# Last angles in halves, turned rows and input projection by pairs of batches, one table set for sine and SiLU, ahead of the state-space loop

## The chip, the core and the metric

The kernel runs on one core of one Trainium2 chip. The metric is the time of one execution on the device in microseconds (us), taken as the median of several runs. A core has five engines with an instruction stream each: TensorE (PE, matrix multiply; weight loads are listed apart as PEld), VectorE (DVE), ScalarE (ACT), GpSimd (POOL) and SyncE (SP, which issues the transfers here). Each runs its stream strictly in program order; they wait for each other on semaphores. Matmul results land in eight banks of PSUM, 512 float32 columns each, numbered 0 to 7.

## The reference, cut to what matters

Two decoder layers on `x` (8 batches of 128 tokens, 128 wide), each with three residual blocks followed by a layer norm. Layer 0: a gated delta-rule attention, a cross-attention on a context, and a feed-forward with a sine. Layer 1: a state-space block, a cross-attention with folded projections, and a gated feed-forward. The change lies between the sine feed-forward and the state-space block:

```python
# layer 0, feed-forward: 512 hidden features
hidden = x @ W1 + b1
imag = w_imag * sin(theta + hidden * 0.1)
phase = cos(theta) * w_real + sin(theta) * w_imag
x = layernorm(x + relu(hidden + phase * imag * 0.1) @ W2 + b2)
# layer 1, state-space block: 256 inner features, 16 states
xp, z = split(x @ W_in + b_in)
u = silu(xp)
Bm, Cm = split(u @ W_x + b_x)
dt = softplus(u @ W_dt + b_dt)
# scan over the 128 tokens: h = h * exp(dt * A) + dt * u * B ; y = h . C + D * u
y = y * silu(z)
x = layernorm(x + y @ W_out + b_out)
```

## The kernel before

Every engine's stream is written out by hand, with waits on named semaphores (`wait_ge`), so the order in the source is the order on the engine. The 8 batches are worked in two halves of four, g = 0 and g = 1; a half has 4 x 128 = 512 columns, one bank.

**The sine feed-forward.** The hidden features are made in four blocks k = 0 to 3, each of two parts m = 0, 1 of 512 columns: blocks 0 and 1 are the features of half 0, blocks 2 and 3 those of half 1. PE writes block k to two banks (`s3_banks` = 0, 4, 6, 2 is the first of each). ACT's `angle(k)` turns them into turns (angle by 2 pi) in `s3_ang[:, k]`. The sine wants its argument within one turn, so DVE's `fraction(k)` takes the fractional part in two operations over 1024 columns: an add of the constant ROUND, and a subtraction of the whole part. ACT's `sine(k)` takes the sine in place, and DVE's `gate3(k)` combines it with the hidden features. `rectified` applies the relu, PE's `project3(g, bank)` multiplies by W2 and adds the residual in a bank.

**The norm between.** For a half, DVE's `landed(3, g, bank)` waits for the projection and takes mean and variance (`bn_stats`, `bn_aggr`, then `veps`), POOL's `power(3, g)` raises variance plus epsilon to the power -0.5 (one small instruction on 128x4, tile `rstd`), and DVE's `normal(3, g, bank)` writes the four normalized batches to `xrow`, one instruction each.

**Into the state-space block.** PE's `turn_half(3, 0)` transposes the four batches as each is normalized, all to one bank. ACT's `columns_out(3, 0)` copies that bank to `xcol` in one instruction. PE's `project4` multiplies by W_in, once for each of the two halves of the inner features (n = 0, 1), to banks 4 and 5. ACT's `inner(n, ...)` applies SiLU to `u4`. PE's `steps(0, bank, n)` makes the step sizes and `narrow` the rows B and C. Then come the pieces of softplus on ACT (abs, exp, relu, ln) and DVE, and the loop over 64 steps q: DVE's `drive_of` (L681) and `scan_of` (L688), ACT's `fading`, POOL's `read_out` (L1052), PE's `widen_b` (L1751) and `accumulate` (L1767). A normalized half 1 follows inside the loop.

**Tables.** ACT's functions come in table sets, and an `ACT_TABLE_LOAD` changes the set. `table_of(f)` issues a tiny activation of function f, so that the load for it stands where that call stands. Where a function that isn't in the current set comes without such a call, the compiler puts the load ahead of it.

The line numbers of the profile are those of the kernel before; the changed kernel's are 10 to 23 higher. This is what DVE does before:

```python
            fraction(2)
            landed(3, 0, 0)
            fraction(3)
            normal(3, 0, 0)
            gate3(2)
            gate3(3)
```

## Time and profile before

| | |
|---|---|
| median of 3 runs | 390.78 us (390.59 to 390.94) |
| the profiled execution | 391.07 us, of which 388.8 us are the span from the first to the last instruction |
| busy in the span | PE 318.3 us (82%), DVE 310.2 (80%), ACT 213.7 (55%), POOL 217.0 (56%) |
| mean granted TensorE clock | 0.943 of full speed |

The profiled execution is one run; its time is 0.29 us above the median, and 2.27 us of it lie outside the span. Busy shares are means over very different stages: until some 119 us the first attention and the cross-attention, until 157 us the sine feed-forward and the beginning of the state-space block, until about 272 us the loop, and then the last cross-attention and feed-forward. In a timeline row, merged instructions stand as one with their count (for PE two records make one float32 matmul of the forms here, save the 128-column transposes, which have one), and the bracket says how long the engine was idle just before and what released it. Neighbouring instructions of an engine overlap by some hundredths of a us.

### The profile page before, as it was taken

What the parts mean: (1) busy time and instruction counts of PE and PEld (TensorE: products, weight loads), DVE (VectorE), ACT (ScalarE), POOL (GpSimd) and SP (SyncE); (2) the same over time, 40 slices, a digit from 0 to 9 for tenths busy, and PEclk for the clock granted to TensorE, in tenths of its full rate; (3) what the DMA queues carried; (4) which work ended last, traced back from release to release, by engine and by line L of the source; (5) the groups of instructions that cost most, each with busy time, mean ns of one, the idle gap of its engine ahead of it and who ended that gap; (6) DMA issues with size and microseconds to landing.
All of it is one profiled execution on the core that took longest, in us unless ns stands there. A gap on an engine that the chain in (4) does not pass through costs nothing. (4 is left out here: it accounts for less than half of the span.)

```text
span 388.8 us, 5449 instructions
## 1 busy us (share of the span) xinstructions
PE 318.3 (82%) x1750; PEld 234.4 (60%) x1750; DVE 310.2 (80%) x630; ACT 213.7 (55%) x468; POOL 217.0 (56%) x223
## 2 busy tenths in 40 slices
PE   5636929779768889867976997978899989999992
PEld 2432419778546465634434985555698857989872
DVE  0799999998676977989999999999958724763934
ACT  2726131222135859857759636787465657675741
POOL 3399999997133050478999999888602610100111
PEclk9956968999999999979998799999999999999998
DMA  8900000000000001334534443543200000000010
GB/s 238 418 35 1 0 3 0 2 1 2 0 0 2 1 0 36 124 112 132 158 121 156 141 142 118 155 136 135 81 3 0 0 2 0 3 1 2 0 29 27
DMA packets 11522, 24.43 MB, mean 63 GB/s; under 512 B 1231, under 2 KB 2255, under 8 KB 11239
## 3 DMA queue, kind: packets, MB, share of 16 engines
q1 hardware_dynamic: 11495, 24.09, 18.9%
q8 instruction: 14, 0.23, 0.2%
q14 instruction: 13, 0.11, 0.1%
HBM read 23.50 MB, written 0.59 MB: 62 GB/s over the span
## 5 line engine op out<-in xcount | busy, mean ns | idle before, releaser
L1052 POOL TENSOR_TENSOR arena<-arena 128x512 f32<-128x512 f32 x63 | 80.1, 1281 | 27.8 <-DVE arena L688 25.8
L688 DVE TENSOR_TENSOR_SCAN arena<-arena,ps 128x512 f32<-128x512 f32 x64 | 77.3, 1209 | 0.1
L1311 ACT ACTIVATE arena<-arena,neg_a 128x508 f32<-128x508 f32 x64 | 43.2, 712 | 9.2 <-DVE arena L688 7.1
L681 DVE TENSOR_TENSOR ps<-arena,ps 128x512 f32<-128x512 f32 x64 | 43.2, 676 | 1.2 <-PE ps L1751 1.1
L1767 PE MATMUL ps<-first_in,arena 128*128 128x128 f32 x256 | 41.4, 286 | 3.2 <-POOL arena L1052 3.1
L1093 POOL TENSOR_TENSOR rstd<-veps,mhalf 128x4 f32<-128x4 f32 (+2 forms) x6 | 4.8, 810 | 68.8 <-DVE veps L803 35.8
L1585 PE MATMUL ps<-arena,first_in 128*128 128x128 f32 (+1 forms) x256 | 31.9, 287 | 12.7 <-POOL arena L926 12.7
L715 DVE TENSOR_REDUCE arena<-ps 128x2 f32<-128x496 f32 x32 | 21.4, 668 | 25.1 <-PE ps L1813 25.0
L1767 PEld LDWEIGHTS ps<-first_in,arena 128*128 128x128 f32 x256 | 33.0, 147 | 13.7 <-POOL arena L1052 6.5
L1585 PEld LDWEIGHTS ps<-arena,first_in 128*128 128x128 f32 x256 | 30.8, 201 | 14.0 <-issue 8.1
L1751 PE MATMUL ps<-arena,pick_wide 96*128 96x512 bf16 x64 | 25.5, 404 | 16.7 <-DVE arena L688 16.2
L1361 ACT ACTIVATE first_in<-ps 128x256 f32<-128x256 f32 x32 | 12.4, 387 | 33.2 <-PE ps L1839 33.1
L1347 ACT ACTIVATE arena<-ps,arena 128x248 f32<-128x248 f32 x64 | 29.4, 472 | 0.9 <-DVE arena L715 0.8
L1751 PEld LDWEIGHTS ps<-arena,pick_wide 96*128 96x128 bf16 x64 | 6.4, 100 | 35.4 <-DVE arena L688 32.6
L1813 PE MATMUL ps<-kvT,arena 128*128 128x248 f32 x96 | 24.2, 375 | 0.0
L939 POOL TENSOR_TENSOR rstd<-veps,mhalf 128x4 f32<-128x4 f32 x8 | 8.6, 1074 | 24.4 <-DVE veps L701 16.3
L1188 ACT ACTIVATE arena<-arena 128x64 f32<-128x64 f32 x15 | 6.2, 413 | 28.5 <-DVE arena L539 28.5
L926 POOL TENSOR_TENSOR arena<-arena 128x512 f32<-128x512 f32 x16 | 20.6, 1289 | 0.3
L1850 PEld LDWEIGHTS ps<-fold_vo,first_in 128*128 128x128 f32 x128 | 18.4, 191 | 3.8 <-ACT first_in L1361 2.1
L1850 PE MATMUL ps<-fold_vo,first_in 128*128 128x128 f32 x128 | 19.6, 279 | 1.2 <-ACT first_in L1361 0.5
L724 DVE TENSOR_TENSOR arena<-arena 128x496 f32<-128x496 f32 x28 | 19.6, 700 | 1.0
L1355 ACT ACTIVATE arena<-ps 128x512 f32<-128x512 f32 x32 | 19.2, 600 | 1.2 <-PE ps L1827 0.2
(290 smaller groups left out, 809.8 us busy)
## 6 DMA issues: line engine op xcount, KB each, us to landing
arena<-c_rows_dram SPq DMA_DIRECT2D x64, 256.0 KB, 3.2
fold_in<-in_fold_dram SPq DMA_DIRECT2D x1, 2056.0 KB, 11.9
late_in<-in_late_dram SPq DMA_DIRECT2D x1, 1423.5 KB, 17.2
early_in<-in_early_dram SPq DMA_DIRECT2D x1, 921.5 KB, 13.7
xres<-in_x_dram SPq DMA_DIRECT2D x1, 512.0 KB, 14.2
kv_ctx<-in_context_dram SPq DMA_DIRECT2D x1, 480.0 KB, 7.8
first_in<-in_first_dram SPq DMA_DIRECT2D x1, 465.0 KB, 3.9
rows_in<-in_rows_dram SPq DMA_DIRECT2D x1, 384.0 KB, 14.7
```

The costliest lines, as they stand in the source:

```text
L681: tt(chain(q), dtu[:, n, cols(g)], chain(q), ALU.mult).then_inc(S("drive"), 1)
L688: nc.vector.tensor_tensor_scan(hist[:, q % NBUF], fade[:, q % NFADE], chain(q), 0.0, ALU.mult, ALU.add).then_inc(S("scan"), 1)
L715: nc.vector.tensor_reduce(s5_max[:, u % 2], sim, AX.X, ALU.max, negate=True).then_inc(S("sim_max"), 1)
L926: tt(prod_s[:, :, c % NR].rearrange("p j t i -> p t i j"), Qg[:, c].unsqueeze(2).to_broadcast([P, C, DH, DH]), state[:, c].unsqueeze(1).to ...
L1052: tt(seen[:, q % NBUF], hist[:, q % NBUF], c_wide[:, q % NBUF], ALU.mult).then_inc(S("read_out"), 1)
L1311: act(fade[:, q % NFADE].rearrange("p (b t) -> p b t", t=T)[:, :, 1:], dt[:, n, cols(g)].rearrange("p (b t) -> p b t", t=T)[:, :, 1:], ACT ...
L1347: act(s5_p[:, u % 2, h], sim_bank(u)[:, h * 256:h * 256 + KV], ACT.Exp, bias=s5_max[:, u % 2, h:h + 1], accum_out=s5_den[:, u % 2, h:h + 1 ...
L1585: ins = mm(bank(6 + c // NR)[:, at:at + n_c * C * DH], ident, pr[:, j, c % NR:c % NR + n_c].rearrange("p c t i -> p (c t i)"), start=(n == ...
L1751: mm(chain(q), pick[:, s], bc_parts[0:96, cols(g)], start=True, stop=True).then_inc(S("b_mm"), 1)
L1767: ins = mm(y_bank(p // NS)[:, b * T:(b + 1) * T], seen[:, p % NBUF, b * T:(b + 1) * T], ident, is_transpose=True, start=False, stop=last a ...
L1813: ins = mm(sim_bank(u)[:, i * 256:i * 256 + KV], s5_q[b // HB][h + i][:, b % HB * T:(b % HB + 1) * T], kvT[:, b], start=True, stop=True)
L1850: ins = mm(out5_bank(b), s5_z[:, u % 4, i * T:(i + 1) * T], fold_vo[:, h + i], start=(h + i == 0), stop=(h + i == XH - 1))
```

## The change

Five edits. DVE: the last block of angles is made fractional by its two halves of columns, one half ahead of `landed(3, 0, 0)`, one in the old place. ACT: a `table_of(Silu)` stands ahead of the first sine, and the one after the last sine is gone; the last sine is taken in two halves. PE and ACT: the four transposes of half 0 go by pairs to banks 4 and 1, and each pair is copied to `xcol` by itself. PE: W_in is applied to one pair after the other, 256 columns at a time. PE, ACT and DVE: the first step sizes go to bank 0 in place of bank 3, so that their matmuls wait for the gates up to the sixth only, while `narrow` behind them waits for all eight; the filler matmuls `stay_awake` behind them write bank 3 in place of bank 0.

```diff
--- before.py
+++ after.py
@@ -633,13 +633,23 @@
                     ts(s3_act[1][:, f], s3_ang[:, k, m * 512:(m + 1) * 512], W("b1")[:, f:f + 1], 0.0,
                        ALU.add, ALU.max).then_inc(S("act3_second"), 1)
 
+            def last_fraction(m):
+
+                ve.wait_ge(S("angle"), 7 + m)
+                ve.wait_ge(S("fraction"), 2 + m)
+                at = slice(m * 512, (m + 1) * 512)
+                whole, turns = s3_t[:, 1, at], s3_ang[:, 3, at]
+                then(ts(whole, turns, ROUND, None, ALU.add))
+                stt(turns, whole, ROUND, turns, ALU.subtract, ALU.subtract).then_inc(S("fraction"), 1)
+
             fraction(0)
             fraction(1)
             gate3(0)
             gate3(1)
             fraction(2)
+            last_fraction(0)
             landed(3, 0, 0)
-            fraction(3)
+            last_fraction(1)
             normal(3, 0, 0)
             gate3(2)
             gate3(3)
@@ -667,7 +677,7 @@
             b_low(0)
             ve.wait_ge(S("dt_lost"), 1)
             ve.wait_ge(S("dt_relu"), 1)
-            then(tt(dt[:, 0, h0], bank(3), dtu[:, 0, h0], ALU.subtract))
+            then(tt(dt[:, 0, h0], bank(0), dtu[:, 0, h0], ALU.subtract))
             ve.wait_ge(S("dt_log"), 1)
             tt(dt[:, 0, h0], bank(5), dt[:, 0, h0], ALU.add).then_inc(S("dt"), 1)
             ve.wait_ge(S("dt"), 1)
@@ -1227,6 +1237,7 @@
             act(na, na, ACT.Copy, scale=-1.0).then_inc(S("neg_a"), 1)
             mixed0(0)
             ac.wait_ge(S("theta"), 1)
+            table_of(ACT.Silu)
             act(s3_sin, s3_th, ACT.Sin).then_inc(S("theta_sin"), 1)
             turned0(1)
             mixed0(1)
@@ -1263,9 +1274,14 @@
             rectified(1)
             angle(3)
             sine(2)
-            sine(3)
-            columns_out(3, 0)
-            table_of(ACT.Silu)
+            for m in range(2):
+                ac.wait_ge(S("fraction"), 4 + m)
+                ins = act(s3_ang[:, 3, m * 512:(m + 1) * 512], s3_ang[:, 3, m * 512:(m + 1) * 512], ACT.Sin, scale=-2 * PI_F)
+            ins.then_inc(S("sine"), 1)
+            for m in range(2):
+                ac.wait_ge(S("turned"), 2 * B + 2 * (m + 1))
+                act(xcol[:, 2 * m:2 * m + 2], bank(4 - 3 * m)[:, 0:2 * T].rearrange("p (b t) -> p b t", b=2),
+                    ACT.Copy).then_inc(S("xcol"), 1)
 
             def inner(n, g, k):
 
@@ -1315,10 +1331,10 @@
             for n in range(NH):
                 inner(n, 0, 4 + n)
             table_of(ACT.Exp)
-            step_abs(0, 3, bank(4))
+            step_abs(0, 0, bank(4))
             step_exp(0, bank(4))
             rows_b(0, 2)
-            step_relu(0, 3, bank(3))
+            step_relu(0, 0, bank(0))
             table_of(ACT.Ln)
             ac.wait_ge(S("dt_lost"), 1)
             step_log(0, bank(5), bank(4))
@@ -1715,10 +1731,16 @@
                 mm(bank(k), W("w_in")[:, n * P:(n + 1) * P], xcol[:, g * HB:(g + 1) * HB],
                    start=True, stop=True).then_inc(S(sem), 1)
 
-            turn_half(3, 0)
-            pe.wait_ge(S("xcol"), 5)
-            for n in range(NH):
-                project4(n, 0, 4 + n, "u_mm")
+            for b in range(HB):
+                pe.wait_ge(S("normed"), normed(3, b + 1))
+                turn(bank(4 - b // 2 * 3)[:, b % 2 * T:(b % 2 + 1) * T], xrow[:, 1, b], ident).then_inc(S("turned"), 1)
+            for m in range(2):
+                pe.wait_ge(S("xcol"), 5 + m)
+                for n in range(NH):
+                    ins = mm(bank(4 + n)[:, 2 * m * T:2 * (m + 1) * T], W("w_in")[:, n * P:(n + 1) * P], xcol[:, 2 * m:2 * m + 2],
+                             start=True, stop=True)
+                    if m:
+                        ins.then_inc(S("u_mm"), 1)
             wx = W("w_x").rearrange("p (n s) -> p n s", n=NH)
             wdt = W("w_dt").rearrange("p (n d) -> p n d", n=NH)
 
@@ -1728,11 +1750,12 @@
             def steps(m, k, n):
                 return mm(bank(k), wdt[:, n, m % 2 * P:(m % 2 + 1) * P], u4[:, n, cols(m // 2)], start=(n == 0), stop=(n == NH - 1))
 
-            pe.wait_ge(S("gated"), 2 * NF)
+            pe.wait_ge(S("gated"), 6)
             for n in range(NH):
                 pe.wait_ge(S("u_in"), n + 1)
-                ins = steps(0, 3, n)
+                ins = steps(0, 0, n)
             ins.then_inc(S("dt_mm"), 1)
+            pe.wait_ge(S("gated"), 2 * NF)
             for n in range(NH):
                 ins = narrow(0, 2, n)
             ins.then_inc(S("xdbl_mm"), 1)
@@ -1884,7 +1907,7 @@
             for n in range(NH):
                 ins = steps(1, 6, n)
             ins.then_inc(S("dt_mm"), 1)
-            stay_awake(4, 0)
+            stay_awake(4, 3)
             pe.wait_ge(S("diag_d"), NH)
             for q in range(NQ):
                 if q + 2 < NQ:
@@ -1901,7 +1924,7 @@
                     pe.wait_ge(S("dt_relu"), 2)
                     turn_half(3, 1)
                 if q == 6:
-                    pe.wait_ge(S("xcol"), 6)
+                    pe.wait_ge(S("xcol"), 7)
                     pe.wait_ge(S("fold_vo"), 2)
                 if q in (6, 7):
                     project4(q - 6, 1, q - 2, "u_mm")
```

On DVE, between the fractions of block 2 and the gates of blocks 2 and 3. Before:

```order
L620 TENSOR_SCALAR arena<-arena 128x1024
L621 SCALAR_TENSOR_TENSOR arena<-arena 128x1024
L416 BN_STATS stats<-ps 128x6 x4
L419 BN_AGGR mv<-stats 128x2 x4
L396 TENSOR_SCALAR veps<-mv 128x4
L620 TENSOR_SCALAR arena<-arena 128x1024
L621 SCALAR_TENSOR_TENSOR arena<-arena 128x1024
L425 TENSOR_SCALAR xrow<-ps,mv,rstd 128x128 x4
L628 SCALAR_TENSOR_TENSOR arena<-arena,s_cf,ps 128x512 x4
```

And now (L642 and L643 are the two operations of `last_fraction`):

```order
L620 TENSOR_SCALAR arena<-arena 128x1024
L621 SCALAR_TENSOR_TENSOR arena<-arena 128x1024
L642 TENSOR_SCALAR arena<-arena 128x512
L643 SCALAR_TENSOR_TENSOR arena<-arena 128x512
L416 BN_STATS stats<-ps 128x6 x4
L419 BN_AGGR mv<-stats 128x2 x4
L396 TENSOR_SCALAR veps<-mv 128x4
L642 TENSOR_SCALAR arena<-arena 128x512
L643 SCALAR_TENSOR_TENSOR arena<-arena 128x512
L425 TENSOR_SCALAR xrow<-ps,mv,rstd 128x128 x4
L628 SCALAR_TENSOR_TENSOR arena<-arena,s_cf,ps 128x512 x4
```

The last 1024-column pair (L620, L621) has become two 512-column pairs, one of them ahead of the statistics (L416).

On ACT, from the last angles (L1240) to the first piece of softplus (L1287). Before:

```order
L1240 ACTIVATE arena<-ps,s_bias 128x512 x2
L1252 ACTIVATE arena<-arena 128x1024 x2
L1111 ACTIVATE xcol<-ps 128x512
L1105 ACT_TABLE_LOAD
L1105 ACTIVATE table<-first_in 128x1
L1273 ACTIVATE arena<-ps,late_in 128x512 x2
L1105 ACT_TABLE_LOAD
L1105 ACTIVATE table<-first_in 128x1
L1287 ACTIVATE ps<-ps,late_in 128x512
```

And now, from the last angles (L1251) on:

```order
L1251 ACTIVATE arena<-ps,s_bias 128x512 x2
L1263 ACTIVATE arena<-arena 128x1024
L1279 ACTIVATE arena<-arena 128x512 x2
L1283 ACTIVATE xcol<-ps 128x256 x2
L1289 ACTIVATE arena<-ps,late_in 128x512 x2
L1115 ACT_TABLE_LOAD
L1115 ACTIVATE table<-first_in 128x1
L1303 ACTIVATE ps<-ps,late_in 128x512
```

The load and the one-column activation between the copy to `xcol` and the two SiLU (L1273 before, L1289 now) are gone; the sine (L1252) of block 3 has become two of 512 columns (L1279), and the copy (L1111) two of 256 (L1283). The load ahead of the first sine is now followed by one such one-column activation.

On PE, from the transposes to `steps` (L1729 before, L1751 now) and `narrow` (L1726, L1748), with the semaphores that they wait for. Before:

```order
L1541 MATMUL ps<-first_in,xrow 128x128 [waits normed] x4
L1715 MATMUL ps<-xcol,late_in 128x512 [waits xcol]
L1715 MATMUL ps<-xcol,late_in 128x512
L1729 MATMUL ps<-arena,late_in 128x512 [waits u_in,gated]
L1729 MATMUL ps<-arena,late_in 128x512 [waits u_in]
L1726 MATMUL ps<-arena,late_in 32x512 x2
L1604 MATMUL ps<-xres,first_in 128x512 [waits residual]
```

And now:

```order
L1736 MATMUL ps<-first_in,xrow 128x128 [waits normed] x4
L1740 MATMUL ps<-xcol,late_in 128x256 [waits xcol]
L1740 MATMUL ps<-xcol,late_in 128x256
L1740 MATMUL ps<-xcol,late_in 128x256 [waits xcol]
L1740 MATMUL ps<-xcol,late_in 128x256
L1751 MATMUL ps<-arena,late_in 128x512 [waits u_in,gated]
L1751 MATMUL ps<-arena,late_in 128x512 [waits u_in]
L1748 MATMUL ps<-arena,late_in 32x512 [waits gated]
L1748 MATMUL ps<-arena,late_in 32x512
```

Two projections of 512 columns (L1715) have become four of 256 (L1740), the third with a wait of its own, all four behind the fourth transpose; the first `narrow` has a wait.

## Rows read from the trace of the kernel before

**Rows 1.** Page, the 40 slices: granted TensorE clock in tenths of full speed, 9.72 us each

```profile
...
PEclk9956968999999999979998799999999999999998
```

**Rows 2.** Windows: us, then busy us (xinstructions) of five engines, granted clock, DMA share, GB/s

```profile
...
139.20:147.00 7.80, 6.60 (x24) 3.84 (x23) 7.63 (x21) 3.84 (x6) 5.38 (x6) 1.00 0.00 0
170.00:172.00 2.00, 1.19 (x7) 0.70 (x5) 2.00 (x3) 0.82 (x2) 2.00 (x3) 0.51 0.07 24
195.00:271.70 76.70, 64.78 (x370) 45.53 (x369) 76.12 (x101) 52.51 (x98) 70.16 (x63) 0.96 0.43 138
271.70:388.80 117.10, 105.60 (x627) 87.93 (x625) 71.22 (x183) 67.78 (x205) 21.85 (x27) 0.98 0.04 12
```

**Rows 3.** Page, costliest groups: total busy, mean ns of one | idle before, releaser

```profile
...
L688 DVE TENSOR_TENSOR_SCAN arena<-arena,ps 128x512 f32<-128x512 f32 x64 | 77.3, 1209 | 0.1
...
L1361 ACT ACTIVATE first_in<-ps 128x256 f32<-128x256 f32 x32 | 12.4, 387 | 33.2 <-PE ps L1839 33.1
```

**Rows 4.** Timeline: start us, us, engine line op xcount [idle before <-releaser]

```profile
...
136.32 1.25 ACT L1240 ACTIVATE arena<-ps,s_bias 128x512 f32<-128x512 f32 x2
...
138.91 3.62 PE L1535 MATMUL ps<-first_in 128*128 128x256 f32 x16
139.12 0.89 DVE L416 BATCH_NORM_STATS2 stats<-ps 128x6 f32<-128x128 f32 x4 [2.32 <-PE ps L1698]
...
140.54 0.69 DVE L620 TENSOR_SCALAR arena<-arena 128x1024 f32<-128x1024 f32 x1
140.71 1.40 POOL L939 TENSOR_TENSOR rstd<-veps,mhalf 128x4 f32<-128x4 f32 x1 [0.28 <-DVE veps L396]
141.26 1.23 DVE L621 SCALAR_TENSOR_TENSOR arena<-arena 128x1024 f32<-128x1024 f32 x1
...
142.41 1.36 DVE L425 TENSOR_SCALAR xrow<-ps,mv,rstd 128x128 f32<-128x128 f32 x4
142.52 1.06 ACT L1252 ACTIVATE arena<-arena 128x1024 f32<-128x1024 f32 x1 [4.02 <-DVE arena L621]
...
142.87 1.28 PE L1541 MATMUL ps<-first_in,xrow 128*128 128x128 f32 x4 [0.33 <-DVE xrow L425]
...
143.80 2.72 DVE L628 SCALAR_TENSOR_TENSOR arena<-arena,s_cf,ps 128x512 f32<-128x512 f32 x4
...
144.19 0.60 ACT L1111 ACTIVATE xcol<-ps 128x512 f32<-128x512 f32 x1 [0.61 <-PE ps L1541]
144.80 1.28 ACT L1105 ACT_TABLE_LOAD   x1
...
144.84 1.98 PE L1715 MATMUL ps<-xcol,late_in 128*128 128x512 f32 x4 [0.69 <-ACT xcol L1111]
...
146.21 1.34 ACT L1273 ACTIVATE arena<-ps,late_in 128x512 f32<-128x512 f32 x2
146.56 1.68 DVE L633 TENSOR_SCALAR arena<-arena,late_in 128x512 f32<-128x512 f32 x4
...
147.02 1.95 PE L1729 MATMUL ps<-arena,late_in 128*128 128x512 f32 x4 [0.20 <-ACT arena L1273]
...
149.01 0.66 ACT L1287 ACTIVATE ps<-ps,late_in 128x512 f32<-128x512 f32 x1
```

**Rows 5.** Instructions by tile, rstd: ns min/median/max

```profile
...
L939 POOL TENSOR_TENSOR rstd<-veps,mhalf x8: 1018/1029/1397, 103.3 to 297.1; 128x4 f32<-128x4 f32 x8
```

**Rows 6.** Timeline, around 92 us, the end of the first attention stage

```profile
...
92.01 1.05 DVE L327 TENSOR_TENSOR arena<-arena 128x512 f32<-128x512 f32 x1
92.06 0.97 POOL L957 TENSOR_SCALAR s_th<-late_in 128x4 f32<-128x4 f32 x1
```

**Rows 7.** Timeline, around 119 us, the load ahead of the first sine

```profile
...
118.92 1.28 ACT L1230 ACT_TABLE_LOAD   x1
...
120.58 0.60 ACT L1211 ACTIVATE arena<-ps 112x512 f32<-112x512 f32 x1 [0.17 <-PE ps L1649]
```

**Rows 8.** Timeline, DVE in the state-space loop

```profile
...
177.38 0.69 DVE L681 TENSOR_TENSOR ps<-arena,ps 128x512 f32<-128x512 f32 x1 [0.82 <-PE ps L1751]
```

## Prediction

> **What bounds the kernel now.** I read the windows first, then who waits in the stretch that the change touches. In the loop the bound is DVE: from 195 to 271.7 us it is busy for 76.12 of 76.70 us [rows 2], and its 64 scans waited 0.1 us in all [rows 3]. Behind the loop it is PE, busy for 105.60 of 117.10 us [rows 2]. Neither is touched, and both start from what came before, so any time won or lost ahead of the loop should arrive at the end unchanged. Ahead of it, from 139.2 to 147.0 us, DVE is busy for 7.63 of 7.80 us [rows 2], but only its first half stands in the way of others: the gates behind the normal are not waited for at once. PE's 6.60 us [rows 2] hold 3.62 us of filler matmuls at 138.91 [rows 4]. What sets the end here is a chain that goes from engine to engine. In the timeline [rows 4] it runs: statistics at 139.12 (DVE sat idle for 2.32 us before them), then the power on POOL at 140.71 beside DVE's last fractions (L620, L621); the normal at 142.41 (L425); transposes from 142.87; one copy to `xcol` at 144.19; W_in from 144.84; SiLU at 146.21; step sizes (L1729) at 147.02; the absolute value (L1287) at 149.01. From there on the order on every engine is as before.
>
> I call the start of the normal N. Before, N = 142.41 and the absolute value starts at N + 6.60. The change can win in both parts.
>
> **Part one: N, by the angles in halves.** The 1024-column pair at 140.54 and 141.26 ends at 142.49 and is what the normal waits for: it starts at 142.41, neighbours on an engine overlapping by 0.08 [rows 4]. A half costs 0.42 for the first operation (1.68 us for four scalar operations of 512 columns, L633) and 0.68 for the second (2.72 for four of L628, which read one operand from PSUM; the 1.23 us of L621 halved with the same fixed part gives the same within 0.02) [rows 4]. The early half goes into the idle 2.32 us: its angle, the first of the two of L1240, is there at about 137.0, so it ends at about 138.2, 0.9 us before the statistics. It costs nothing; without that cover it would cost 1.1. The late half runs from 140.54 to about 141.68. DVE could thus start the normal at 141.60.
>
> Now POOL is late. Its power ran from 140.71 to 142.11 [rows 4]; it took 1.40 us where the median of eight is 1.03 [rows 5]. The excess, 0.37, fits a wait behind L620, which ended at 141.23: the power would have asked for its operands some 0.15 us after its start. That such waits exist is seen in [rows 6], where a POOL operation on 128x4 stood for 0.97 us and ended with the DVE operation beside it. With the half operation ending at 140.96 the wait shrinks to 0.1 and the power ends at 140.71 + 1.13 = 141.84; with nothing in its way it ends at 141.74, with the old 1.40 at 142.11. Adding 0.03 for the signal, N = 141.87, bounds 141.77 and 142.14. Part one wins **0.54 us** (0.27 to 0.64).
>
> The Trainium skill (SBUF — State Buffer, Two separate sides) says that VectorE and GpSimd share a pair of ports by an exclusive lock, held for a whole instruction, taken by a VectorE operation in a two-port mode or by one with two SBUF inputs. The 1.40 and the 0.97 agree with that. It speaks against this change in one way: L621 and L643 have two SBUF inputs, and if L643 gets the ports first, the power waits for its end; the first rival below prices this.
>
> **Part two: from N to the absolute value.** The four normals end 0.34 us apart (1.36 for four). Before, the transposes start at N + 0.46 and take 0.32 each, the last ends at N + 1.74, the copy runs from N + 1.78 to N + 2.38, and W_in starts at N + 2.43 [rows 4]. By pairs: the second transpose ends at about N + 1.10, the copy of 256 columns costs 0.39 [rows 3], so the first pair is in `xcol` at N + 1.53. All four transposes stand ahead of W_in on PE, the last ending at N + 1.74, but starting at N + 1.42, so W_in starts at N + 1.58 to 1.74. I take 1.58, since pipelined neighbours overlap. The second copy starts at N + 1.78 and ends at N + 2.17, ahead of the third projection. ACT is free for them: the late half of the sine costs less than the whole 1.06 [rows 4] and starts at 141.7, so it is done by about 142.4, and the first copy is due at 143.0.
>
> W_in itself costs the same columns. Two projections of 512 took 1.98 us (L1715) [rows 4], four passes of 0.43 and 0.26 until the result is there. The filler of 256 columns took 3.62 for 16 passes (L1535), 0.21 each with the same 0.26. So eight passes take 1.94; the first SiLU's operand is complete after six, at N + 1.58 + 1.52 = N + 3.10, the second's at N + 3.52. ACT starts SiLU at about N + 3.15, where it started at N + 3.80 before. Here the table counts: before, the load (1.28 us from 144.80) and the tiny activation behind it (0.13, until 146.21) ended later than the first projection, ready at 144.84 + 0.86 + 0.26 = 145.96. Alone, the removed load would win those 0.25 for the first SiLU, and almost nothing for the second (its operand was ready at 146.82, and it started at about 146.88). With the pairs, both move.
>
> From the first SiLU on, the distances hold: its 0.67, then the step sizes 0.14 later, 1.95 us for them, and on ACT 2.80 us from the start of the first SiLU to the absolute value (146.21 to 149.01, with two SiLU of together 1.34 and the table of Exp between) [rows 4]. ACT and PE reach this point together, at N + 5.95, where it was N + 6.60. The step sizes now wait for the gates up to the sixth (about N + 2.8), and `narrow` for all eight (N + 4.11; the four gates take 2.72 from N + 1.39), both ahead of need. Had bank 3 and the wait for eight stayed, the gates would still end at N + 4.11, at most 0.15 after the first SiLU at N + 3.82: that edit alone is worth 0.15 at most. Part two wins **0.65 us** (0.49 with W_in at N + 1.74).
>
> The Trainium skill (ScalarE: Activation LUTs, What ACT_TABLE_LOAD costs) gives 1.28 us for a load, as here, plus 1.38 for a drain. No drain of that size shows here: SiLU followed the load's end by 0.13 [rows 4]. By the page's 2.66 us ACT would be freed for longer, but the sum would stay, since PE's projection is what is waited for then.
>
> **What is added.** The load ahead of the first sine now has the tiny activation behind it, 0.13. ACT had 0.17 idle before its next copy (L1211) [rows 7], so ACT loses nothing. POOL's coefficients from that sine, and behind them on its stream the power of the block before, can be up to 0.13 later, and the second norm with it, unless PE covers it. I take **-0.05** (0 to -0.13). Bank 0 in place of 3, and the filler in the other bank, cost nothing, since reads and writes keep their sizes and order.
>
> **The sum.** 0.54 + 0.65 - 0.05 = 1.14 us. The profiled execution's 391.07 (388.8 in the span, 2.27 around it) would become 389.93; it stood 0.29 over the median, so for the median of 390.78 I say **389.65 us**. The likeliest case's own range is 389.4 to 390.0 (0.27 + 0.49 - 0.13 = 0.63 takes all bounds at once and belongs to the second rival).
>
> **The rivals.**
> - *The power falls behind L643.* If POOL asks after 140.96, the second operation has the operands' way, until 141.68; what the power had left at 141.23 before (until 142.11, 0.88) then ends at 142.56. N = 142.59, 0.18 later than before. 0.65 - 0.18 - 0.05 = 0.42 won: 390.35. For it: the margin, 0.25 us after POOL's start, is small. Against it: in the same place before, the power got through between L620 and L621. Chance 0.13.
> - *Both parts win at their lower ends*, the power staying at 1.40 us and W_in behind the last transpose: 0.63 to 0.76 won, 390.05 to 390.15. For it: nothing shows that the 1.40 came from L620. Chance 0.12.
> - *TensorE's clock falls elsewhere.* From about 170 us the granted clock was 0.51 [rows 2], 1.2 GHz in place of 2.4, for nearly one slice [rows 1], after a stretch in which PE had waited much; DVE waited for PE 0.82 us at 177.38 [rows 8]. If this interval shrinks as the stages shift, 0.8 us or a little more is won on top: about 388.8. Chance 0.06.
> - *It is slower.* The one mechanism that could do it is that same low clock in the chain before the loop, between 143 and 149 us: eight passes of 0.21 and four of 0.43 on the chain would double, +3.4 us, and 392 to 393 would result. It decides from about 2 us, half of the interval. Against it: the clock was 1.00 from 139.2 to 147.0 [rows 2], and PE waits less there after the change. Chance 0.05.
> - That the table's load isn't saved is excluded: the compiled order shows one load fewer and none between sine and SiLU.
>
> **How the numbers follow.** The forecast has 0.64. A measurement of this kernel tells about 0.2% (0.78 us) from no change. Faster by more than that: nearly all of the forecast, the clock's case and a little of the second rival, 0.71. Within: the first rival and most of the second, 0.23. Slower: 0.06. The range 389.1 to 390.4 holds forecast and both rivals, and leaves out the two of the clock.
>
> **What would show it.** The early fractions stand in the gap at about 137.1 to 138.2, and the statistics still start at 139.1. The power takes 1.0 to 1.15 us, and the normal starts at 141.9. The copies start 0.64 apart, W_in at N + 1.6, SiLU at N + 3.15, the absolute value at N + 5.95, that is at 147.8. The first scan, and then every later stage, is earlier by the same 1.1 us. It is wrong if the power is longer than 1.3 us, if the chain behind 149 us gives time back, or if the low clock moves.

## Result, and the profile after

The changed kernel takes **388.47 us** (median of 6 runs, 387.89 to 389.17), the kernel before 390.73 us in the same comparison (6 runs): a ratio of 0.9945, 95% interval 0.993 to 0.996, that is 1.6 to 2.7 us less. The forecast was 389.65 with a range of 389.1 to 390.4: the direction was right, the gain (2.26 us in place of 1.13) twice as large, and the time lies below the range. The profiled execution took 388.73 us, with a span of 386.5 in place of 388.8.

The chain ahead of the loop, from the timeline of the changed kernel (columns as in [rows 4], which hold the same places of before):

```profile
...
137.01 0.43 DVE L642 TENSOR_SCALAR arena<-arena 128x512 f32<-128x512 f32 x1 [0.22 <-ACT arena L1251]
...
137.47 0.69 DVE L643 SCALAR_TENSOR_TENSOR arena<-arena 128x512 f32<-128x512 f32 x1
...
139.10 0.89 DVE L416 BATCH_NORM_STATS2 stats<-ps 128x6 f32<-128x128 f32 x4 [0.94 <-PE ps L1714]
...
140.53 0.43 DVE L642 TENSOR_SCALAR arena<-arena 128x512 f32<-128x512 f32 x1
140.69 1.14 POOL L949 TENSOR_TENSOR rstd<-veps,mhalf 128x4 f32<-128x4 f32 x1 [0.28 <-DVE veps L396]
140.99 0.69 DVE L643 SCALAR_TENSOR_TENSOR arena<-arena 128x512 f32<-128x512 f32 x1
...
141.87 1.36 DVE L425 TENSOR_SCALAR xrow<-ps,mv,rstd 128x128 f32<-128x128 f32 x4 [0.18 <-POOL rstd L949]
...
142.36 1.26 PE L1736 MATMUL ps<-first_in,xrow 128*128 128x128 f32 x4
...
143.01 0.38 ACT L1283 ACTIVATE xcol<-ps 128x256 f32<-128x256 f32 x1 [0.67 <-PE ps L1736]
...
143.45 1.99 PE L1740 MATMUL ps<-xcol,late_in 128*128 128x256 f32 x8
143.65 0.38 ACT L1283 ACTIVATE xcol<-ps 128x256 f32<-128x256 f32 x1 [0.25 <-PE ps L1736]
145.05 1.27 ACT L1289 ACTIVATE arena<-ps,late_in 128x512 f32<-128x512 f32 x2 [1.01 <-PE ps L1740]
...
145.88 1.95 PE L1751 MATMUL ps<-arena,late_in 128*128 128x512 f32 x4 [0.44 <-ACT arena L1289]
...
147.88 0.66 ACT L1303 ACTIVATE ps<-ps,late_in 128x512 f32<-128x512 f32 x1
```

N, the start of the normal, is 141.87 where it was 142.41; the power took 1.14 us in place of 1.40. The first half of the fractions stands in the old gap, and the statistics start where they did, with 0.94 us idle ahead of them in place of 2.32. From N: W_in 1.58 later (2.43 before), SiLU 3.18 (3.80), the absolute value 6.01 (6.60).

The remaining gain of these two profiles lies in the loop. Below are the starts of a few of its scans in the two profiles, q counted from 0 (merged from the timelines; the third column is the difference):

```
 q    before   after    gain
 0    157.46   156.32   1.14
 8    175.35   174.18   1.17
 9    177.99   175.89   2.10
10    179.70   177.60   2.10
14    186.53   184.60   1.93
35    225.14   223.20   1.94
36    227.93   225.64   2.29
62    278.24   275.95   2.29
```

At the first scan the gain is the forecast's 1.14. It jumps by 0.93 at q = 9, falls by 0.17 up to q = 14, jumps by 0.35 at q = 36, and holds in between and from there to the end. The page of the changed kernel shows the granted clock (40 slices of 9.66 us; compare [rows 1]):

```profile
...
PEclk9955968999999999988997999999999999999997
```

and the windows show it finer (columns as in [rows 2]):

```profile
...
170.00:174.00 4.00, 4.00 (x13) 2.39 (x14) 3.76 (x5) 2.98 (x4) 4.00 (x5) 0.58 0.45 125
174.00:178.00 4.00, 3.30 (x17) 1.64 (x16) 4.00 (x6) 3.95 (x5) 4.00 (x4) 1.00 0.37 102
178.00:182.00 4.00, 2.49 (x14) 1.76 (x12) 4.00 (x5) 2.81 (x6) 3.87 (x4) 0.77 0.63 196
182.00:186.00 4.00, 4.00 (x16) 1.86 (x15) 3.94 (x6) 2.79 (x6) 4.00 (x4) 0.80 0.38 105
```

Before, TensorE ran at half clock (1.2 GHz) from about 170 to 177 us, and DVE waited for it, 0.82 us at 177.38 alone [rows 8]. In this execution of the changed kernel the low clock lasted from about 170 to 173.4 and came again from 180.2 to 183.7. Of the waits for TensorE in front of the drive one of 0.24 us is left. The jump at q = 36 comes long after another stretch of 6.8 us at half clock, which both have: it ended at about 217.9 before and at 214.4 now. Before, DVE waited 0.38 us for TensorE at 226.7, now it doesn't; what ties this wait to a low clock is not shown.

### The profile page after: what moved, and what is told of

The parts are those of the page before. It is cut to its first block and busy times, and to the rows that moved or that the text cites. A ratio compares the mean times of both kernels' runs of the same rounds, so it can differ in the third digit from the quotient of the medians.

```text
span 386.5 us, 5462 instructions
## 1 busy us (share of the span) xinstructions
PE 318.1 (82%) x1754; PEld 235.0 (61%) x1754; DVE 310.5 (80%) x632; ACT 212.7 (55%) x469; POOL 216.7 (56%) x223
```

## Experiments

For the runs below, the span of each profile is cut at the start of the statistics (L416), at scan 0, at scan 36 and at scan 62. Behind scan 0 all kernels have one order, save the fillers of the awake ones. Indented lines are further executions of the kernel above them. The profiles come from several chips.

```
                    statistics  to      to      to      to
                    start       scan 0  q = 36  q = 62  the end  span
kernel before       139.12      18.34   70.47   50.31   110.56   388.8
  before_again      137.76      19.61   69.36   50.31   110.56   387.6
  before_look1      139.18      18.35   68.89   50.31   110.57   387.3
  before_look2      139.09      18.34   70.55   50.30   110.52   388.8
awake_before        138.22      19.60   69.35   50.30   110.53   388.0
before_filled       139.52      18.34   68.92   50.31   110.51   387.6
  filled_look1      138.32      18.34   69.94   50.29   110.51   387.4
  filled_look2      139.69      18.34   68.94   50.30   110.53   387.8
table_only          138.26      18.15   70.46   50.31   110.52   387.7
halves_only         139.19      17.81   69.03   50.30   110.47   386.8
all_but_halves      139.26      17.75   69.06   50.30   110.53   386.9
changed kernel      139.10      17.22   69.32   50.31   110.55   386.5
  after_again       138.38      17.21   68.88   50.30   110.53   385.3
  after_look1       139.44      17.21   69.28   50.31   110.56   386.8
  after_look2       138.43      17.21   69.01   50.31   110.54   385.5
awake_after         138.08      17.22   68.92   50.89   110.49   385.6
  awake_filled      138.18      17.21   68.93   50.31   110.47   385.1
after_old_table     139.24      17.60   69.16   50.31   110.49   386.8
after_bank3         137.78      17.40   70.44   50.31   110.47   386.4
after_delayed       139.21      18.45   70.40   50.30   110.54   388.9
```

**Both parts by themselves.** `halves_only` is the kernel before with the fractions and the last sine in halves; `all_but_halves` is the changed kernel without them, its reverse. On the kernel before:

```diff
             fraction(2)
+            last_fraction(0)
             landed(3, 0, 0)
-            fraction(3)
+            last_fraction(1)
...
-            sine(3)
+            for m in range(2):
+                ac.wait_ge(S("fraction"), 4 + m)
...
```

> The kernel before with the last fractions and the last sine in halves, nothing else. Chain: the normal at 141.87 in place of 142.41, the power 1.14 in place of 1.40 us, every distance behind it as before, the first scan at 156.9 (0.54 earlier). Theory: the time is 0.54 us lower, plus or minus what the low clock stretches in the loop do, about 390.2, within 389.2 to 390.6. Rival (parts need each other, ScalarE is what is waited for): first scan earlier by less than 0.2.

> The changed kernel with the last fractions and the last sine whole again: pairs, one table set and bank 0 stay. The normal at 142.4 as before, SiLU 3.2 us behind it in place of 3.8, the absolute value 6.0 in place of 6.6, the first scan 0.6 earlier, at 156.85. Theory: 0.6 us lower, plus or minus the low clock stretches, about 390.1 (389.0 to 390.5). Rival (the halves free ScalarE, and without them the late sine, until 143.6, holds up the first copy, due at 143.5): 0.5 or less.

Measured: 389.63 us (12 runs; ratio 0.9967, 0.995 to 0.9984) and 389.34 us (0.997, 0.9955 to 0.9984). On the way to scan 0 the first wins 0.53 us (17.81 against 18.34), the second 0.59 (17.75); together 1.12, which is what the whole change wins there. `halves_only`, timeline:

```profile
...
140.61 0.43 DVE L642 TENSOR_SCALAR arena<-arena 128x512 f32<-128x512 f32 x1
140.78 1.14 POOL L949 TENSOR_TENSOR rstd<-veps,mhalf 128x4 f32<-128x4 f32 x1 [0.27 <-DVE veps L396]
...
141.95 1.36 DVE L425 TENSOR_SCALAR xrow<-ps,mv,rstd 128x128 f32<-128x128 f32 x4 [0.18 <-POOL rstd L949]
...
145.75 1.34 ACT L1286 ACTIVATE arena<-ps,late_in 128x512 f32<-128x512 f32 x2
...
148.56 0.66 ACT L1300 ACTIVATE ps<-ps,late_in 128x512 f32<-128x512 f32 x1
```

The power is short again, 1.14 us, beside the half operation, and 1.40 in `all_but_halves` beside the whole one. So the parts add up, and neither needs the other. The medians are 1.1 and 1.4 us under that of the kernel before (390.72), each twice its share of the chain. The intervals just leave out the shares of the chain alone, so each half seems to bring some of the part beyond it.

**The pieces of part two.** `table_only` moves the SiLU table ahead of the first sine and nothing else; `after_old_table` is the changed kernel with the tables as before; `after_bank3` is the changed kernel with the step sizes in bank 3 and their wait for all eight gates. The first diff is `table_only` on the kernel before (`after_old_table` is its reverse on the changed kernel), the second `after_bank3` on the changed kernel, its fillers back in bank 0 too:

```diff
+            table_of(ACT.Silu)
             act(s3_sin, s3_th, ACT.Sin).then_inc(S("theta_sin"), 1)
...
             columns_out(3, 0)
-            table_of(ACT.Silu)
```

```diff
-            pe.wait_ge(S("gated"), 6)
+            pe.wait_ge(S("gated"), 2 * NF)
...
-                ins = steps(0, 0, n)
+                ins = steps(0, 3, n)
```

> The kernel before with the one table set alone: SiLU no longer waits for its load. The first SiLU at N + 3.6 in place of 3.80 (W_in's first result), the second at N + 4.45 as before, the absolute value at N + 6.5 to 6.6 where the clock is full. Theory: 0 to 0.1 us on the chain, and the low stretch near 144 us may still come: within 0.3 of the kernel before. Rival (the table is the larger part of the gain): the absolute value at N + 6.2 or earlier.

> The changed kernel with the old tables: a load ahead of the first sine and one behind the last copy, ahead of SiLU. The second copy ends at N + 2.16, the load and its activation take 1.41, SiLU at N + 3.58 in place of 3.18, the absolute value at N + 6.4 in place of 6.01. Theory: 0.4 us slower than the changed kernel, about 388.9, first scan at 17.62 us behind the statistics in place of 17.22. Rival (the load costs a drain of over 1 us beside it): the absolute value at N + 7 or later.

> The changed kernel with the first step sizes in bank 3 again, so that they wait for all eight gates. The last gate ends at 145.99 and the first SiLU at 145.72 in the changed kernel; the step sizes start at 146.1 in place of 145.88, the absolute value at 148.05 to 148.1, 0.2 later. Theory: 0.1 to 0.25 us slower than the changed kernel on the chain, the first scan at 156.5. Rival (nothing waits there): the first scan at 156.32.

Measured: 390.28 us (ratio 0.9977, 0.9955 to 0.9998), 389.27 (0.9944, 0.9916 to 0.9972) and 389.03 (0.9955, 0.9935 to 0.9974). On the way to scan 0 the table alone wins 0.19, where 0 to 0.1 had been expected; taking it out of the changed kernel costs 0.39, and taking bank 0 and the early wait out costs 0.19. In `table_only` the absolute value comes at N + 6.56, only 0.04 earlier, as expected. But the chain doesn't run through it: the step sizes start at N + 4.42 in place of 4.61, `narrow` behind them is earlier by the same 0.19, and a later activation of ACT (L1282, the rows B) waits for `narrow`:

```profile
...
149.80 0.68 ACT L1282 ACTIVATE arena<-ps,late_in 32x512 f32<-32x512 f32 x1 [0.43 <-PE ps L1726]
```

`after_bank3`, timeline:

```profile
...
143.72 1.27 ACT L1289 ACTIVATE arena<-ps,late_in 128x512 f32<-128x512 f32 x2 [1.02 <-PE ps L1740]
...
144.72 1.98 PE L1751 MATMUL ps<-arena,late_in 128*128 128x512 f32 x4 [0.60 <-DVE arena L628]
...
146.74 0.66 ACT L1303 ACTIVATE ps<-ps,late_in 128x512 f32<-128x512 f32 x1 [0.23 <-PE ps L1751]
```

There the step sizes (L1751) wait 0.60 us for DVE's gates, as expected. In `after_old_table` SiLU starts 3.59 us behind N, right behind the load and its small activation, which began when the second copy ended; nothing of a drain shows:

```profile
...
142.00 1.36 DVE L425 TENSOR_SCALAR xrow<-ps,mv,rstd 128x128 f32<-128x128 f32 x4 [0.18 <-POOL rstd L949]
...
143.78 0.38 ACT L1282 ACTIVATE xcol<-ps 128x256 f32<-128x256 f32 x1 [0.25 <-PE ps L1736]
144.19 1.28 ACT L1115 ACT_TABLE_LOAD   x1
...
145.59 1.25 ACT L1289 ACTIVATE arena<-ps,late_in 128x512 f32<-128x512 f32 x2
...
148.40 0.66 ACT L1303 ACTIVATE ps<-ps,late_in 128x512 f32<-128x512 f32 x1
```

**The loop with TensorE kept busy.** Nine filler matmuls (`stay_awake(n, bank)` issues n of 256 columns, whose results nobody reads) in the steps where TensorE waits, in both kernels (`awake_before`, `awake_after`; `awake_filled` is the latter once more):

```diff
+                if q in (1, 3):
+                    pe.wait_ge(S("dt_relu"), 2)
+                    stay_awake(2, 6)
+                if q == 5:
+                    pe.wait_ge(S("fold_vo"), 2)
+                    stay_awake(2, 4)
                 if q == 4:
                     pe.wait_ge(S("dt_relu"), 2)
                     turn_half(3, 1)
+                    pe.wait_ge(S("fold_vo"), 2)
+                    stay_awake(3, 4)
```

> The kernel before, with nine filler matmuls of 256 columns on TensorE in the loop's steps 1, 3, 4 and 5, where TensorE waits, ahead of the place where the granted clock fell (170 to 177 us). Nothing ahead of the loop is changed. Theory (the gain beyond 1.14 us is VectorE's waiting for a half-clock TensorE in the loop): no low clock between 160 and 200 us, the waits of 0.27 and 0.82 us at 174.7 and 177.4 gone, some 1.1 us faster than the kernel before, about 389.6; the distance between scans 4 and 10 falls from 11.57 to about 10.5 us. Rival (the clock has no share, the gain comes from the changed order itself): no gain, or a loss for the fillers, 390.7 or more.

> The changed kernel with the same nine filler matmuls. Theory: with the clock full in both, the two differ by the 1.14 us of the chain ahead of the loop, plus 0.35 at most if the later low stretch near 211 us stays as it is, so 388.1 to 388.5 here and 1.1 to 1.5 below the kernel before with fillers; the first scan at 156.3. Rival (the changed order wins inside the loop too): 2.2 us below the kernel before with fillers, about 387.4 to 388.5 with the other at 390.7.

> The changed kernel with the nine fillers in the loop once more, to see whether the low stretch near 170 us stays away in another execution. Theory: no low stretch between 160 and 200 us, the 34 steps from scan 0 to scan 10 in 20.9 us, 387.7 to 388.3. Rival (its absence was a matter of the one execution): a low stretch of 3.4 us or more there, and the time of the changed kernel.

Measured: 389.86 us (ratio 0.9982, 0.9965 to 0.9999), 387.81 (0.9936, 0.9915 to 0.9956) and 388.21 (0.992, 0.989 to 0.995). `awake_filled` holds the clock through the first forty microseconds of the loop, where the changed kernel has 0.92 over the same window; first line `awake_filled`, then, in a fence of its own, the changed kernel:

```profile
...
156.00:200.00 44.00, 37.67 (x189) 22.05 (x187) 42.82 (x60) 31.02 (x48) 38.38 (x33) 1.00 0.44 125
```

```profile
...
156.00:200.00 44.00, 36.29 (x174) 21.47 (x173) 42.55 (x60) 32.03 (x50) 37.08 (x32) 0.92 0.42 126
```

Both executions of this kernel went from scan 0 to scan 36 in 68.92 and 68.93 us, with the clock full up to 200 us; that is the shortest seen, to 0.05. `awake_before` missed its forecast in its profile: the stretch near 170 us was gone, but another of the same length stood from 179 to 185.8, so that the loop took 69.35; and it held a surprise ahead of the loop:

```profile
...
144.00:148.00 4.00, 4.00 (x6) 1.68 (x7) 3.30 (x7) 3.02 (x5) 0.23 (x1) 0.60 0.00 0
170.00:174.00 4.00, 3.97 (x22) 2.54 (x21) 4.00 (x6) 2.01 (x4) 4.00 (x4) 1.00 0.24 81
...
182.00:186.00 4.00, 4.00 (x13) 2.47 (x12) 3.73 (x6) 2.66 (x4) 4.00 (x4) 0.53 0.44 157
```

TensorE was at half clock from about 144.7 to 148.3 us, right in the chain, and the absolute value came at N + 7.87 in place of 6.60. The two kernels with fillers stand 2.05 us apart in one comparison (389.86 and 387.81), and `awake_filled` in another stands 1.65 under the first; the theory had 1.1 to 1.5, the rival 2.2. With low stretches left in `awake_before`, this distance doesn't decide between them. The next experiments ask how the stretches are spread.

**Both kernels once more.**

> The kernel before, unchanged, as a null and to see whether the granted clock falls in the same places in another execution. Theory (the low stretches move from execution to execution, and their place sets part of the time): ratio to the kernel before about 1.000, the chain from the normal to the absolute value again 6.60 us where the clock is full, but a low stretch in another place or of another length, and single times spread over 1.5 us or more. Rival (the low stretch from 170 to 177 us belongs to this kernel's order): the same stretch, within 1 us of the same place and 6.8 us long.

> The changed kernel, unchanged. The normal to the absolute value 6.01 us and the power 1.14 where the clock is full; 388.5 us, 2.2 below the kernel before. Theory (the gain beyond the chain is systematic, though by way of the clock): the median stays 1.8 to 2.7 below the kernel before. Rival (the gain beyond 1.14 us is luck of a few executions): 0.9 to 1.6 below, about 389.5.

Measured: 390.70 us (12 runs; 0.9998, 0.9983 to 1.0013) and 388.31 (6 runs; 0.9931, 0.9908 to 0.9954). The gain over 1.14 us is no luck of one comparison: the medians stand 2.26 us apart in the first and 2.31 in this one (the kernel before 390.62 over 24 runs), or 2.39 with `before_again` as the kernel before. But the low stretches do move. `before_again` has one of 3.4 us near 144, like `awake_before`:

```profile
...
144.00:148.00 4.00, 4.00 (x7) 1.62 (x6) 2.85 (x6) 2.72 (x5) 0.00 (x0) 0.58 0.00 0
170.00:174.00 4.00, 3.12 (x10) 1.70 (x9) 4.00 (x5) 2.01 (x3) 4.00 (x5) 0.66 0.28 83
...
182.00:186.00 4.00, 4.00 (x14) 2.17 (x13) 3.74 (x5) 2.66 (x4) 4.00 (x5) 0.64 0.44 151
```

```profile
...
141.06 1.36 DVE L425 TENSOR_SCALAR xrow<-ps,mv,rstd 128x128 f32<-128x128 f32 x4
...
143.49 3.37 PE L1715 MATMUL ps<-xcol,late_in 128*128 128x512 f32 x4 [0.69 <-ACT xcol L1111]
...
146.89 0.69 ACT L1273 ACTIVATE arena<-ps,late_in 128x512 f32<-128x512 f32 x1 [1.02 <-PE ps L1715]
...
149.00 0.65 ACT L1287 ACTIVATE ps<-ps,late_in 128x512 f32<-128x512 f32 x1
```

W_in takes 3.37 us in place of 1.98 [rows 4], the second SiLU waits 1.02 us for it, and the absolute value comes at N + 7.94. In the loop the low clock then lasted 3.4 us from about 171 and 3.4 near 182, as it did in the changed kernel's first profile. Scan 0 to scan 36 took 69.36 us, not 70.47. So the rival, that the stretch from 170 to 177 us belongs to the order, is out.

**The same start with the new order.** `after_delayed` is the changed kernel with scratch work on DVE ahead of the normal (twice 1024 columns, whose result nobody uses):

```diff
             last_fraction(1)
+            for _ in range(2):
+                ts(s3_t[:, 0], s3_t[:, 1], ROUND, None, ALU.add).then_inc(S("vector_step"), 1)
+                count[0] += 1
+                join()
             normal(3, 0, 0)
```

> The changed kernel with two more operations of 1024 columns on VectorE ahead of the normal (1.4 us of work on scratch), so that the normal starts at about 143.0 and the absolute value at about 149.0, as in the kernel before; all of the new order stays. Theory (all of the gain, the part in the loop too, comes from the loop starting earlier): the first scan at 157.4 and 390.7 us, no different from the kernel before within 0.5. Rival (the new order, with less waiting of TensorE between the transposes and W_in, keeps the clock up whatever the start): 389.6 or less.

Measured: 389.72 us (12 runs; 0.9985, 0.9965 to 1.0004). Its profile is that of the kernel before again: scan 0 at 157.66, the low clock from 170 to 177 us, 70.40 us to scan 36. That alone would speak for the start of the loop as what sets its length. The median doesn't: it is 1.0 us under the forecast of 390.7 and 0.1 over the rival's bound, with an interval that allows both. And the other profiles speak against the start: `after_bank3`, which has all of the new order but the bank, began its scans earliest of all twenty, at 155.18, and took 70.44 us to scan 36, with the wait of the kernel before:

```profile
...
175.08 0.69 DVE L691 TENSOR_TENSOR ps<-arena,ps 128x512 f32<-128x512 f32 x1 [0.81 <-PE ps L1773]
```

`table_only` began at 156.41 and took 70.46, the changed kernel in `after_look1` at 156.65 and took 69.28. Neither the new order nor an early start keeps the long form of the loop away.

**Does waiting between transposes and W_in bring the stretch near 144 us?**

```diff
             turn_half(3, 0)
+            stay_awake(1, 1)
             pe.wait_ge(S("xcol"), 5)
```

> The kernel before with one filler matmul of 256 columns (0.45 us) on TensorE between the four transposes and W_in, where TensorE waits 0.69 us for the copy. Seen so far: in two of three profiles with the old order ahead of the loop the granted clock fell from about 144 to 148 us and put the absolute value at N + 7.9 in place of 6.6; in none of seven with the new order or half of it. Theory (that stretch comes from TensorE's waiting there, which the change took away): no low clock between 140 and 155 us, the absolute value at N + 6.6, and the median 0.4 to 1.0 below the kernel before, 389.7 to 390.3. Rival (it comes from elsewhere, and its absence in seven is luck): the stretch shows again or the median is within 0.3 of the kernel before.

> The kernel before with one filler matmul between the transposes and W_in, one look. Theory: no low stretch between 140 and 155 us, also where the statistics start early, the absolute value at N + 6.60. Rival: the stretch is there with an early start, the absolute value at N + 7.9.

> The same kernel as in the first look, with one filler between transposes and W_in. No low stretch between 140 and 155 us, the absolute value at N + 6.60; the rival is the stretch there all the same.

> The kernel before, one look. Theory (the low stretch near 144 us belongs to the old order in those executions whose statistics start by about 138.4 us): there with an early start, the absolute value then at N + 7.9; not there with the statistics at 139.1, the absolute value at N + 6.60. Rival (no tie): either way round.

> The kernel before, a second look. With the statistics by about 138.4 us the low stretch near 144 us and the absolute value at N + 7.9, otherwise neither; the rival is that the two are not tied.

> The changed kernel, one look. 17.22 us from the statistics to the first scan, no low clock between 140 and 155 us. Theory: 68.9 to 69.4 us from scan 0 to scan 36, where the four profiles of the kernel before have 68.9 to 70.6. Rival (the loop is as long as before on the mean): 70.0 or more in one of the two looks.

> The changed kernel, a second look: 17.22 us from the statistics to the first scan, 68.9 to 69.4 from scan 0 to scan 36; the rival is 70.0 or more in one of the two looks.

Measured: `before_filled` 389.98 us (0.9984, 0.9956 to 1.0012); the labels with `look` have one execution each, 389.33 and 390.22 with the filler, 389.71 and 391.26 without, 389.20 and 387.78 for the changed kernel. None of the three profiles with the filler has the stretch, none of the ten in which W_in goes by pairs, and two of the seven with W_in whole and no filler have it. Both of these are among the executions whose statistics started early (137.76 and 138.22 us): there it is two of three with the old wait (`table_only`, at 138.26, is without), and none of six with the filler or the pairs. With so few that is a hint and no proof, and `before_filled`'s median doesn't decide it.

The two single executions of the kernel before are the clearest pair for the loop: the same code, the statistics at 139.18 and 139.09, the low clock over at 174 in one and at 177 in the other, and 68.89 against 70.55 us to scan 36. Each fence ends with the second of the two W_in projections of half 1, which stand in the loop's steps 6 and 7:

```profile
...
170.00:174.00 4.00, 3.12 (x10) 1.61 (x9) 4.00 (x6) 2.00 (x4) 4.00 (x5) 0.57 0.32 85
174.00:178.00 4.00, 3.20 (x18) 1.89 (x16) 4.00 (x6) 3.96 (x5) 4.00 (x4) 1.00 0.43 118
...
174.72 1.02 PE L1715 MATMUL ps<-xcol,late_in 128*128 128x512 f32 x2
```

```profile
...
170.00:174.00 4.00, 3.12 (x9) 1.56 (x8) 4.00 (x5) 2.00 (x4) 4.00 (x5) 0.51 0.36 92
174.00:178.00 4.00, 4.00 (x16) 2.42 (x15) 2.85 (x4) 3.96 (x5) 4.00 (x4) 0.63 0.36 114
...
175.31 1.83 PE L1715 MATMUL ps<-xcol,late_in 128*128 128x512 f32 x2
```

What decides between the short and the long form shows here. TensorE works this projection off ahead of the matmul (`widen_b`) that DVE's next drive needs. All twenty profiles fit:

```
profiles                        second projection   DVE's wait behind it   scan 0 to 36
kernel before, before_look2,
table_only, after_bank3,
after_delayed                   1.73 to 1.83 us     0.78 to 0.88 us        70.40 to 70.55
filled_look1                    1.32                0.37                   69.94
the other fourteen              1.02                none                   68.88 to 69.36
```

In the five of the first line the low clock lasted until 19.3 to 19.5 us behind scan 0, in `filled_look1` until 18.5; in the others no low clock lay between 17.4 and 21 us behind it. The same five, and no others, have the extra 0.35 us between scans 34 and 36.

The changed kernel's two took 69.28 and 69.01 us, as expected, and no execution with a late start had the stretch near 144 us. But both new executions of the kernel before started late, so that the tie of that stretch to an early start was tested only on its easy side.

## Why the prediction was right about the chain and wrong about the time

- *Part one* was right, term by term. Forecast 0.54, measured 0.53 (from the statistics to N, 3.29 us before, 2.75 to 2.77 after). The power shrank to 1.14 us (forecast 1.13) and was in DVE's way as worked out. The first rival, the power behind L643, did not come in any of the ten profiles with the halves, and neither did the second, its 1.40 us staying.
- *Part two* was right too: forecast 0.65, measured 0.59. W_in started at N + 1.58 as taken, SiLU at N + 3.18 (forecast 3.15), the absolute value at N + 6.01 (5.95). The early wait for the gates was put at 0.15 at most and is worth 0.19. The table's removal alone was put at 0.25 for the first SiLU and almost nothing for the second; alone it is worth 0.19 at scan 0, by way of the step sizes and `narrow`, and within the pairs 0.39.
- *What is added* was put at -0.05 and was nothing: the second norm started 0.07 later (122.97 in place of 122.90), and its copy to `xcol` at 124.80 in both. Statistics at 139.10, before 139.12.
- *The step that failed* is the first one: "any time won or lost ahead of the loop should arrive at the end unchanged". From scan 36 on it did, to 0.1 us but for one execution. Ahead of it, it didn't, because the loop's first part, and in some executions the chain itself, hold stretches at half clock whose place and length change from execution to execution. The window from which the prediction read the loop's bound begins at 195 us [rows 2], behind the part in which the scans gained 0.79 of their 1.15 us. It took the stretch from 170 to 177 us as a fixture of the kernel, put nothing for it into the sum, and gave 0.06 to its changing; that rival, at 388.8, is the one that came nearest. In the profiles the kernel before takes 68.89 to 70.55 us from scan 0 to 36, on the mean of four 69.82, the changed one 68.88 to 69.32, mean 69.12: 0.70 more won. The chain takes 18.34 us in three and 19.61 in one of the four profiles of the kernel before (mean 18.66) and 17.21 or 17.22 in all four of the changed: 1.45 won in place of 1.12. Together 2.15 us, of the 2.3 measured. Of this only the 1.12 is sure to belong to the change: four profiles against four, which overlap, don't tell the 0.70 from chance, and the 0.33 comes from one profile of the four.
- *The slower rival* had its mechanism right and its kernel and size wrong: half clock between 143 and 149 us showed in one execution of the kernel before and one of `awake_before`, and cost 1.3 us there, not 3.4.
- *Two slips* change nothing: of PE's 6.60 us the fillers are 3.33 (they began at 138.91, ahead of the window), and 390.78 less 0.76 is 390.02, not 390.05.

Shown are the chain's 1.12 us and its parts; that the gain beyond them is there in two comparisons; and, in the profiles, what makes most of the difference in the loop's first part: whether the low clock lasts into the second W_in projection. Not shown is why the changed kernel meets less low clock, if it does. For the chain's part there are the waits of TensorE: 0.33 us ahead of the transposes and 0.69 behind them are gone, while the one ahead of the step sizes has grown from 0.20 to 0.44. For the loop's part an earlier start was the idea, and `after_bank3` and `table_only` speak against it.

The clocks of the executions without a kept trace don't settle it either. At the same mean granted clock of the whole span, 0.945, the kernel before has a mean span of 387.56 us (18 executions) and the changed kernel of 385.80 (4); a straight line through all 113 executions of the two on record puts them 2.0 us apart at equal clock, with a standard error of 0.2. So, as far as this mean tells, the changed kernel's gain over 1.12 us is not simply less time at half clock. Either the low stretches lie in places where they cost less, which a mean over the span can't show, or something else has a share. About half of the 2.3 us thus has an open cause.

## What to carry to other kernels

A profile is one execution, also in its clock. Before a low stretch of TensorE's clock is counted as part of a kernel, take two or three profiles and cut them at fixed instructions: what repeats to a hundredth is the kernel, what moves is the clock. Then ask which instruction the low stretch must not reach: here a projection of 1.02 us at full clock, and 1.8 at half, decided over 0.8 us of DVE's waiting. In a chain from engine to engine, cheap wins are work that delays a short instruction's neighbour (halve it, put one half in a gap) and whole-bank handovers (hand over by pairs); here they added up as worked out from durations and starts, to 0.1 us. Where the measured gain is twice the sum, don't credit the rest to the change's mechanism before further executions and variants have been asked.

## What the runs showed of the hardware beyond that

- A POOL operation of 128x4 took 1.03 us undisturbed, 1.14 with a DVE operation of 0.43 us over its start, 1.40 with one of 0.69, and 1.63 in `after_delayed`, where scratch operations also lay over its end. There it ended at 142.43, when the first of the two scratch operations was over (1.46 us for both, from 141.70). That fits an operation which can wait at its end as at its start; one row is all that shows it:

```profile
...
140.63 0.43 DVE L642 TENSOR_SCALAR arena<-arena 128x512 f32<-128x512 f32 x1
140.80 1.63 POOL L953 TENSOR_TENSOR rstd<-veps,mhalf 128x4 f32<-128x4 f32 x1 [0.27 <-DVE veps L396]
...
141.70 1.46 DVE L654 TENSOR_SCALAR arena<-arena 128x1024 f32<-128x1024 f32 x2
```

  The Trainium skill (SBUF — State Buffer, Two separate sides) says that the shared ports are locked for a whole instruction by whichever starts first, a VectorE operation in a two-port mode or with two SBUF inputs, or a GpSimd operation. That POOL waited for L642 or L620 beside it (1.14 and 1.40 us in place of 1.03) agrees, if these run in a two-port mode, which no row shows. That POOL's own operation holds DVE out for its whole length does not: L643, with two SBUF inputs, ran its usual 0.69 us from 140.99 beside a power that lasted until 141.83.

- Sine and SiLU needed no load between them, and the sine took the same time from the shared set (1.05 us for the 1024 columns of block 2 in both kernels, at 137.46 before and 137.45 now).
- The statistics start up to 1.9 us earlier or later from profile to profile (137.76 to 139.69), and 1.4 us in the kernel before alone. With it goes the clock of the first attention stage: in eight of the nine profiles whose statistics start by 138.43 the fourth slice (29 to 39 us) of the page has 8 tenths, in none of the eleven that start from 139.09 on, which have 5 or 6. `before_again` (137.76) and `before_look1` (139.18):

```profile
...
PEclk9958969999999998988997899999999999999997
```

```profile
...
PEclk9955968999999999989997899999999999999997
```
